# Four attentions over 128-token blocks: the scores of one half of the heads issued beside the shifted scores of the other half, and two products trading places in two of the stages

## The reference, cut to what matters

```python
q = (query @ Wq).reshape(b, nq, H, HD).transpose(0, 2, 1, 3)
k = (key @ Wk).reshape(b, nk, H, HD).transpose(0, 2, 1, 3)
v = (value @ Wv).reshape(b, nk, H, HD).transpose(0, 2, 1, 3)
attn = jnp.einsum('bhqd,bhkd->bhqk', q, k) * HD ** (-0.5)
attn = jax.nn.softmax(attn, axis=-1)
x = jnp.einsum('bhqk,bhkd->bhqd', attn, v)
x = x.transpose(0, 2, 1, 3).reshape(b, nq, H * HD)
return x @ Wo + bo          # then layernorm(x_before + this)
```

## Time and profile before

| | |
|---|---|
| median of 3 runs | 3042.08 us (3035.75 to 3054.31) |
| the profiled execution | 3054.53 us |
| its span, first to last instruction | 3052.6 us |
| PE / PEld busy | 2592.3 us (85%) / 2075.3 us (68%) |
| DVE / ACT / POOL busy | 1428.0 (47%) / 848.5 (28%) / 675.4 (22%) us |
| mean granted TensorE clock | 0.894 of 2.4 GHz |

### The profile page before, as it was taken

One profiled execution on the slowest core, in us unless ns is written; L12 is line 12 of the kernel. 1 busy time (PEld: TensorE's weight loads), 2 busy tenths in 40 slices (PEclk: granted clock), 3 DMA queues, 4 the chain that ended last, 5 costly groups with the idle time before them and its releaser, 6 DMA issues. The chain is left out here.

```text
span 3052.6 us, 53590 instructions
## 1 busy us (share of the span) xinstructions
PE 2592.3 (85%) x20565; PEld 2075.3 (68%) x20565; DVE 1428.0 (47%) x2899; ACT 848.5 (28%) x1462; POOL 675.4 (22%) x1011
## 2 busy tenths in 40 slices
PE   6879998669799898999799899559879969779990
PEld 3857776335688555999588677348568858579990
DVE  3266665775367421121477456431546647621115
ACT  1133332643233210111222234013334424312220
POOL 1832221321122100222112111013101211123331
PEclk9889999889899899999899899669977769889995
DMA  8110000000200001888100200126100000079982
GB/s 321 41 39 1 0 1 21 8 0 1 78 2 2 29 1 69 316 315 299 44 1 0 77 2 2 33 80 186 33 1 2 2 4 2 29 260 325 326 297 84
DMA packets 163710, 254.27 MB, mean 83 GB/s; under 512 B 17760, under 2 KB 124512, under 8 KB 163296
## 3 DMA queue, kind: packets, MB, share of 16 engines
q1 hardware_dynamic: 154336, 230.98, 21.9%
q0 software_dynamic: 9216, 21.06, 2.5%
HBM read 220.35 MB, written 31.13 MB: 82 GB/s over the span
## 5 line engine op out<-in xcount | busy, mean ns | idle before, releaser
L3180 PE MATMUL te_pU<-te_xsT,te_wu 128*128 128x128 f32 x1952 | 235.6, 278 | 1.8 <-DMA te_wg<-in_L_ffn_gate 1.0
L3180 PEld LDWEIGHTS te_pU<-te_xsT,te_wu 128*128 128x128 f32 x1952 | 233.1, 195 | 5.5 <-issue 2.6
L3201 PE MATMUL te_pY<-te_wd,te_hT 128*128 128x256 f32 x976 | 220.8, 379 | 0.0
L2042 PE MATMUL x_pR<-x_kx,x_qx 32*128 32x128 f32 x1536 | 188.5, 305 | 18.5 <-ACT x_kx L2200 13.3
L3201 PEld LDWEIGHTS te_pY<-te_wd,te_hT 128*128 128x128 f32 x976 | 180.9, 190 | 21.8
L2042 PEld LDWEIGHTS x_pR<-x_kx,x_qx 32*128 32x128 f32 x1536 | 154.6, 200 | 48.2 <-issue 43.7
L2252 DVE TENSOR_REDUCE x_mx<-x_pR 128x8 f32<-128x1024 f32 x96 | 117.6, 1225 | 141.0 <-PE x_pR L2042 140.5
L2047 PE MATMUL x_pT<-x_qx,x_kx 32*128 32x128 f32 x1536 | 176.1, 281 | 1.2 <-ACT x_Pr L2167 1.2
L2167 ACT ACTIVATE x_Pr<-x_pT 128x1024 f32<-128x1024 f32 x96 | 98.2, 1023 | 255.6 <-PE x_pT L2047 255.4
L2047 PEld LDWEIGHTS x_pT<-x_qx,x_kx 32*128 32x128 f32 x1536 | 151.9, 196 | 3.0 <-ACT x_Pr L2167 1.7
L1117 PE MATMUL x_pB<-early,x_xlT 128*128 128x384 f32 x384 | 137.5, 502 | 4.7 <-DVE x_qn L1344 3.0
(11 more groups left out here) (618 smaller groups left out, 5805.9 us busy)
## 6 DMA issues: line engine op xcount, KB each, us to landing
te_wu<-in_L_ffn_w_upT SPq DMA_DIRECT2D x39, 1024.0 KB, 5.6
te_wd<-in_L_ffn_w_downT SPq DMA_DIRECT2D x39, 1024.0 KB, 5.7
te_wu<-in_L_ffn_up SPq DMA_DIRECT2D x22, 1024.0 KB, 4.9
te_wg<-in_L_ffn_gate SPq DMA_DIRECT2D x22, 1024.0 KB, 7.0
te_wd<-in_L_ffn_down SPq DMA_DIRECT2D x22, 1024.0 KB, 7.8
moe_first<-in_L_ffn_W SPq DMA_DIRECT2D x8, 1024.0 KB, 8.8
ao_got<-ys_slots SPq DMA_DIRECT2D x12, 512.0 KB, 6.1
xs_slots<-zeros SPq DMA_DIRECT2D x1, 5120.0 KB, 23.5
```

Of the source, the lines that this page charges most:

```text
L2042: return pe.matmul(pR[:, j, c, :], qx[b % 4][g, c, :], kx[b % 4][g, c, :], start=mask is None, stop=mask is None or c == SLOTS16 - 1)
L3180: ins = pe.matmul(out[g][:, m, :], w[:, k, bass.ts(PER * g + m, P)], xsT[:, k, :], start=(k == 0), stop=(k == KD - 1))
L3201: ins = pe.matmul(pY[u][:, 0, :], hT[:, k, :], wd[u][:, k, :], start=(k == 0), stop=(k == KH - 1))
```

## The change

`scores(n, half)` pairs the scores of one half with the shifted scores of the other: the row groups now follow each other as 0, 2, 1, 3 (or 2, 0, 3, 1), two records each. The semaphores, the order of the two exponentials on ACT and of the two `weigh` on DVE are turned round to match. In x2 and x3, `output` moves between the two sets of scores and the next query's projection behind the second set; on ACT the `query` store goes behind the second exponentials, on DVE the `residual` of the output goes between `maximum` 0 and `normalise`. a3 and x1 keep their order apart from the pairing.

```diff
@@ scores(n, half) on PE
                         if live(n):
                             done = score(half, j, c, n)
                         if live(n - 1):
-                            last = shifted_score(half, j, c, n - 1)
+                            last = shifted_score(1 - half, j, c, n - 1)
                 if live(n - 1):
-                    last.then_inc(t_ready[half], 1)
+                    last.then_inc(t_ready[1 - half], 1)
@@ the turn on PE
-                    since(pe, e_done[1], n - 2)
+                    since(pe, e_done[0], n - 2)
                 scores(n, 0)
                 if rope and live(n + 1):
                     projections(n + 1)
                 if live(n - LAG - 3):
                     turn_back(n - LAG - 3)
-                if own and live(n - LAG - 2):
+                if not rope and live(n - LAG - 2):
                     output(n - LAG - 2, n)
-                if kv and live(n + 1):
-                    projections(n + 1)
                 if live(n):
                     since(pe, mx_ready[0], n)
                 if live(n - 1):
-                    since(pe, e_done[0], n - 1)
+                    since(pe, e_done[1], n - 1)
                 scores(n, 1)
-                if own and live(n + 1):
+                if not rope and live(n + 1):
                     projections(n + 1)
                 if rope and live(n + 1):
                     turned_keys(n + 1)
-                if not own and live(n - LAG - 2):
+                if rope and live(n - LAG - 2):
                     output(n - LAG - 2, n + 1)
@@ the turn on ACT
-                    exponentials(n - 1, 0)
+                    exponentials(n - 1, 1)
...
-                if not own and live(n + 1):
+                if rope and live(n + 1):
                     query(n + 1)
                 if live(n - 1):
-                    exponentials(n - 1, 1)
+                    exponentials(n - 1, 0)
+                if not rope and live(n + 1):
+                    query(n + 1)
                 if own and live(n + 1):
-                    query(n + 1)
                     value(n + 1)
@@ the turn on DVE
-                if own and live(n - LAG - 2):
+                if not rope and live(n - LAG - 2):
                     residual(n - LAG - 2)
...
-                if not own and live(n - LAG - 2):
+                if rope and live(n - LAG - 2):
                     residual(n - LAG - 2)
...
                 if penalty is not None and live(n - 1):
+                    weigh(n - 1, 1)
                     weigh(n - 1, 0)
-                    weigh(n - 1, 1)
```

More of the change, by code:

```diff
@@ L2171, in query @@
                 since(act, q_summed if rope else q_ready, b)
-                since(act, t_ready[1], b - 4)
+                since(act, t_ready[0], b - 4)
                 src = q32 if rope else pq
```

## The result

The changed kernel takes 2925.16 us, the median of 4 runs (2920.63 to 2928.77); the kernel before has 3048.19 with its fourth run (3035.75 to 3054.61). The ratio is 0.96 with a 95% interval of 0.9562 to 0.9639: faster by 4%. The forecast was 2928, with a range of 2900 to 2985. The profiled execution took 2928.77 us, 125.8 less than the one before (3054.53).

The account below looks back on a forecast made before the run. PE was taken to fill x2 and x3, and a3 to be slowed by its clock. Savings of 28 + 29 + 14 + 45 = 116 us from the 3042 median gave 2926, rounded to 2928; range 2900 to 2985.

Parts of the forecast that it names:

- A set of 32 records goes from 2.07 to 1.17 us: All stages: paired scores use four row groups instead of two, saving 0.90 us from first record to maximum.
- x1: 28 us: Stage x1: shorter scores and the key's rotation without its wait save 1.73 x 15 turns, plus 2 in first turns.
- x2: 29 us: Stage x2: turn 9.48 instead of 11.24 us, 1.76 x 15 turns, plus 3 for the first turns.
- x3: 14 us: Stage x3: longer way to maximum 1, shorter other half; turn 8.53 instead of 9.29 us, 11 plus 3.
- a3: 45 us: Stage a3: mostly at 2.4 GHz, turn 9.76 instead of 13.70 us, with falls left in a few turns.
- a choice between bounds: Stage a3: gain taken as 45 us between 0 (clock falls as before) and 59 (3.94 x 15).
- The argument against it: Stage a3: PE's 0.71 us wait stands ahead of each clock fall and only grows, since DVE leads.
- The sum: Whole kernel: 28 + 29 + 14 + 45 = 116 us off the median of 3042, giving 2926, rounded to 2928.
- Rivals 1, 2 and 3: 1: a3's clock keeps falling, 2960 (0.22); 2: no four-group overlap, 3040 (0.07); 3: x2/x3 clock falls, 3085 (0.04) or 3040 (0.05).

Follow-up runs that it names:

- experiment 3: The kernel before with the row group changing at every call within a set, still one half and two row groups: 3010.71 us, ratio 0.989.
- experiment 1: The kernel before with the scores paired in all four stages, but output, query projection and residual of x2 and x3 left in place: 2899.29 us, ratio 0.9519.
- experiment 4: The changed kernel with a3 alone unpaired again: 2963.77 us, ratio 0.973 to the kernel before.
- experiments 2: The changed kernel without the pairing, so only the moves of x2 and x3: 3052.52 us, ratio 1.0019 to the kernel before.
- experiment 5: The kernel before with three unused transposes added in each a3 turn, ahead of the second set of scores: 3021.31 us, ratio 0.9922.

## Why the prediction was right

- **A set of 32 records goes from 2.07 to 1.17 us.** Right: 1.21, and 0.90 instead of 1.88 from first to last start. Four row groups work side by side as the column groups do. The Trainium skill's factor of 3.07 for four row tiles ("TensorE: Matmul & The Clock Gate", Part 3) would have given about 1.45, an estimate; here four records take the 0.11 us that two took, which is twice the rate of two groups. No run has one group alone, which is what the page compares with. The matmuls went to four banks of PSUM before as after, so it isn't the number of banks; experiment 3 rules out the mere change of row group from call to call.
- **x1: 28 us.** 31.8. The key's rotation closed up to the maximum as said, and the way from maximum 1 to the next maximum 0 shrank from 7.23 to 5.50, the 1.73 reckoned; the turn is 10.65 for 10.74, and the first turns, at the lower clock, brought more than the 2 us given them (15.04 went to 12.76 and 14.00 to 10.64).
- **x2: 29 us.** 32.2, turn 9.39 for 9.48. The number came out, the account of it only in part. The prediction let DVE set the way to maximum 1 and added the mask's products behind it (4.45 + 4.08 + 0.95). Measured are 4.25 and 5.14 with PE never idle for more than 0.2 us at a time: x2's turn is PE's own work before and after, so it fell by 1.85, about what two sets save. The same 9.40 in experiment 1, where PE has the old order, bears this out. That both reckonings lie so close is luck.
- **x3: 14 us.** 12.9. Maximum 0 to maximum 1 is 4.31 for 4.45, the rest 4.11 for 4.08. DVE just made it, as reckoned: `scaled` ends 0.1 us ahead of the maximum. One step was read otherwise than it came: `attend_values` isn't done while DVE works. It waits 0.99 us for DVE's product, and the turned maxima follow on it 1.32 after maximum 1 instead of 1.30, so that this cost nothing in the sum.
- **a3: 45 us.** 53.4. With the clock up the turn is 9.58 for 9.76, and the falls stayed away but for the first turns and the end. That the clock would hold was a choice between bounds; experiment 4 shows that it was the larger part, 2.9 of the 4.1 us a turn. The argument against it, that PE's waits grow, was true of the waits and wrong of the clock. Why the clock holds once the sets are paired isn't shown; that 45 was near 53.4 is a choice that came out well.
- **The sum.** The terms give 116 and the stages 130.3; x1, x2 and a3 were put too low, a3 by 8 us. Over the kernel as a whole 123.0 arrive (3048.19 - 2925.16). The forecast of 2928 hits to 3 us in part by luck: the gain was 7 us larger than said, and the kernel before 6 us slower than the 3042.08 that it started from.
- **Rivals 1, 2 and 3** did not come about: in a3 the falls ended after the first turns, a set took 1.21 us, and x2 and x3 hold a clock of 1.00 with PE waiting 0.99 us in x3.
- What the prediction did not ask is what the moves are worth. It booked x3's longer way between the maxima (plus 1.06) and the earlier turned maxima (minus 0.92) as one trade. Experiment 1 shows that the pairing alone brings the turned maxima forward too, to 1.37 us behind maximum 1 (2435.20 - 2433.83; before the change 2.22), since scores, exponentials and `attend_values` all end earlier; the moves then only leave their price. The kernel would have been at 2899.

## What to carry to other kernels

Matmuls that use 32 rows of the array are worth pairing so that all four row groups have work at once (here each group wrote to a PSUM bank of its own; sharing one wasn't tried); with two groups, whether two calls of one group follow each other made only 0.2 us of 2.07. After such a gain the limit can be elsewhere, as in x3 and not in x2, so reckon each further move against the new limit and run it apart: work belongs where that engine waits, and a step that was free beside a slow PE is not free between two maxima on DVE. Where a stage runs below 2.4 GHz, ask whether its time is work at all: the same instructions took 13.7 or 10.8 us a turn here, and with a little more work for PE the kernel was 29 us faster.

## What the runs showed of the hardware that was not expected

- A stage can stay in a rhythm in which the clock falls once in each turn, and with the same code in it leave it after eight turns, after nine or not at all (experiments 2 and 4, the kernel before). The kernel before spreads over 3030.51 to 3059.30 us in its 17 runs beside experiments 1 to 3, the changed one over 2921.98 to 2927.24 in its 6.
- With 0.33 us of transposes in a wait of 0.71 a3 left the falling after three turns and stayed at 2.4 GHz (experiment 5); with the wait unfilled it did so after five turns in experiment 3.
- Changing the row group with every call instead of every second call takes 0.2 us off the time from a set's first record to its maximum, with two groups (experiment 3).
